# Both self attentions: ScalarE and VectorE share the copies of the projected values

## What is computed

```python
# first (sa): 16 heads of 16, rotary positions
q, k, v = jnp.split(layernorm(x) @ w_qkv, 3, axis=-1)
q = q * cos + rotate_half(q) * sin          # k likewise
attn = softmax(q @ k.T * scale)             # per sequence and head
x = x + (attn @ v) @ w_out + b_out
# second (sb): 8 heads, 64 wide for q and k, 32 wide for v
q, k = jnp.split(layernorm(x) @ W_qk, 2, axis=-1); v = layernorm(x) @ W_v
attn = softmax(q @ k.T * scale + conv[:, clipped_distance])
x = x + (attn @ v) @ W_out + b_out
```

## Time and profile before

| | us |
|---|---|
| median of 3 runs | 1342.28 (1341.74 to 1342.65) |
| the profiled execution | 1330.97 |
| its span, first to last instruction | 1329.2 |
| TensorE / VectorE / ScalarE / GpSimd busy | 1192.8 / 709.3 / 556.1 / 383.6 |
| value stage of `sa` (first matmul L785 to first of L798) | 862.3 to 875.1 |
| value stage of `sb` | 1182.3 to 1198.0 |

### The profile page before, as it was taken

One profiled execution on the slowest core, in us unless ns is written; L12 is line 12 of the kernel. 1 busy time (PEld: TensorE's weight loads), 2 busy tenths in 40 slices (PEclk: granted clock), 3 DMA queues, 4 the chain that ended last, 5 costly groups with the idle time before them and its releaser, 6 DMA issues. The chain is left out here.

```text
span 1329.2 us, 32322 instructions
## 1 busy us (share of the span) xinstructions
PE 1192.8 (90%) x13863; PEld 1048.1 (79%) x13863; DVE 709.3 (53%) x1127; ACT 556.1 (42%) x907; POOL 383.6 (29%) x339
## 2 busy tenths in 40 slices
PE   4799999999999999999999988796699999278799
PEld 4789889889889899899998977674477778266598
DVE  5555655565565575475475443275564222565732
ACT  4455555555555555555555532214532322111400
POOL 4632332332332342342242210053144000540000
PEclk9899999999999999999999985597989999589989
DMA  6937647647657556566665460190012121414045
GB/s 197 209 85 174 154 102 165 146 116 159 138 132 149 132 140 141 132 145 137 141 149 124 104 128 1 54 363 2 1 68 87 57 64 48 127 28 191 2 176 194
DMA packets 61732, 161.47 MB, mean 121 GB/s; under 512 B 24904, under 2 KB 38296, under 8 KB 58520
## 3 DMA queue, kind: packets, MB, share of 16 engines
q1 hardware_dynamic: 58904, 154.18, 46.0%
q0 software_dynamic: 1536, 4.20, 0.9%
q10 hardware_dynamic: 1152, 1.05, 0.2%
HBM read 70.56 MB, written 9.44 MB: 60 GB/s over the span
## 5 line engine op out<-in xcount | busy, mean ns | idle before, releaser
L366 ACT ACTIVATE xa_pt<-xa_sc 128x1024 f32<-128x1024 f32 (+1 forms) x224 | 212.4, 962 | 151.2 <-PE xa_sc L558 151.1
L412 DVE TENSOR_REDUCE xa_mx<-xa_sc 128x2 f32<-128x804 f32 x256 | 243.4, 991 | 41.4 <-PE xa_sc L542 41.4
L558 PE MATMUL xa_sc<-xa_queries,xa_keys 104*128 104x128 f32 (+1 forms) x1664 | 232.5, 285 | 2.4 <-DVE xa_queries L427 1.8
L558 PEld LDWEIGHTS xa_sc<-xa_queries,xa_keys 104*128 104x128 f32 (+1 forms) x1664 | 206.6, 196 | 21.0 <-issue 8.4
L479 PE MATMUL xa_pj<-xa_ctx_hi,xa_wk 128*128 128x400 f32 (+1 forms) x512 | 157.0, 349 | 0.9 <-DVE xa_qst L440 0.9
L479 PE MATMUL xa_pj<-xa_wv,xa_ctx_hi 128*128 128x256 f32 (+1 forms) x832 | 155.3, 286 | 0.1
L542 PE MATMUL xa_sc<-xa_keys,xa_queries 96*128 96x402 f32 x512 | 138.0, 373 | 13.0 <-DMA xa_keys<-xa_kst_hi 7.3
L569 PE MATMUL xa_op<-xa_pt,xa_values 128*32 128x64 f32 x6656 | 141.8, 228 | 7.7 <-ACT xa_pt L366 3.3
L295 POOL TENSOR_TENSOR xa_ctx_lo<-xa_raw,xa_ctx_hi 128x1600 fp32r<-128x1600 f32 (+1 forms) x32 | 115.9, 3623 | 78.0 <-DVE xa_ctx_hi L405 75.4
L300 POOL TENSOR_TENSOR xa_kst_lo<-xa_wk,xa_kst_hi 128x400 fp32r<-128x400 f32 x64 | 67.3, 1051 | 227.4 <-ACT xa_kst_hi L345 227.4
L479 PEld LDWEIGHTS xa_pj<-xa_wv,xa_ctx_hi 128*128 128x128 f32 (+1 forms) x832 | 126.2, 185 | 8.0 <-issue 6.5
(11 more groups left out here) (286 smaller groups left out, 1736.7 us busy)
## 6 DMA issues: line engine op xcount, KB each, us to landing
xa_keys<-xa_kst_hi SPq DMA_DIRECT2D x256, 200.2 KB, 6.1
xa_keys<-xa_kst_lo SPq DMA_DIRECT2D x128, 200.2 KB, 5.4
xa_raw<-in_ctxT SPq DMA_DIRECT2D x15, 1601.0 KB, 9.0
gf_w<-in_gf_w SPq DMA_DIRECT2D x16, 1024.0 KB, 7.1
moe_ex<-in_moe_ex SPq DMA_DIRECT2D x8, 1088.0 KB, 15.9
xa_queries<-xa_qst SPq DMA_DIRECT2D x96, 32.0 KB, 3.5
moe_slots_in<-in_moe_zero SPq DMA_DIRECT2D x1, 2944.0 KB, 16.4
moe_xs<-moe_slots_in SPq DMA_DIRECT2D x23, 128.0 KB, 2.2
```

Source lines behind the costliest of these rows:

```text
L366: nc.scalar.activation(PT[ptslot(step)][0:rows, 0:nt], SC[bank(step)][0:rows, 0:nt], ACT.Exp, scale=float(D0) ** -0.5).then_inc(ex_done, 1)
L412: nc.vector.tensor_reduce(mx[:, u // 2, 2 * (u % 2):2 * (u % 2) + 2], SC[bank(step)][:, :, 0:MXN], AX.X, ALU.max).then_inc(mx_done, 1)
L558: last = mm(SC[bank(step)][0:rows, kk, a * P:(a + 1) * P], KS[:, 2 * a + h, kt * P:kt * P + rows], QS[b % 2][:, 2 * a + h, :], start=True, ...
```

## The change

In both self attentions VectorE copies the even units only, and ScalarE the odd ones, with a semaphore of its own, `v_free`. Units 1 and 3 come after one half of `lnH` each, units 5 and 7 after the first and the second of `WH`. VectorE makes a half of `lnL` after units 0 and 2. TensorE waits for `v_free` ahead of odd units and for `pj_free` ahead of even ones; `pj_free` now counts 4 and not 8 for the values, so the later thresholds change. Ahead of unit 1 ScalarE also waits for zeros and ones. The diff without its unchanged surroundings:

```diff
-ATTENTION_SEMS = ("ln_hi", "ln_lo", "w_hi", "w_lo", "pj", "pj_free", "rot", ...
+ATTENTION_SEMS = ("ln_hi", "ln_lo", "w_hi", "w_lo", "pj", "pj_free", "v_free", "rot", ...
         def projected(eng, half):
-            eng.wait_ge(pj_free, T + half * (nproj // 2))
+            eng.wait_ge(pj_free, T // 2 + half * (nproj // 2))
             if rope:
                 eng.wait_ge(rot_done, half * (nproj // 4))
+        def values_of(n, e):
+            r_ = slice(e * S, (e + 1) * S)
+            return Vd[r_, 2 * n:2 * n + 2, :, e, 0:dv], PJ[n % 2][r_, 0:D].rearrange("p (b a v) -> p b a v", b=2, v=dv)
...
             for n in range(T):
-                ge(pe, pj_free, n - 1)
+                ge(pe, v_free if n % 2 else pj_free, n // 2)
...
                 n = T + m
-                pe.wait_ge(pj_free, n - 1)
+                pe.wait_ge(v_free if m == 1 else pj_free, T // 2 + max(m - 1, 0))
...
-            for n in range(T):
+            for n in range(0, T, 2):
                 dve.wait_ge(pj, n + 1)
                 for e in range(2):
-                    r_ = slice(e * S, (e + 1) * S)
-                    last = nc.vector.tensor_copy(Vd[r_, 2 * n:2 * n + 2, :, e, 0:dv],
-                                                 PJ[n % 2][r_, 0:D].rearrange("p (b a v) -> p b a v", b=2, v=dv))
+                    last = nc.vector.tensor_copy(*values_of(n, e))
                 last.then_inc(pj_free, 1)
-                if n % 2 and n // 2 < CH:
+                if n // 2 < CH:
                     k = n // 2
...
-                    dve.wait_ge(pj_free, n + 1)
+                    dve.wait_ge(pj_free, T // 2 + m + 1)
...
+            def values(n):
+                act.wait_ge(pj, n + 1)
+                if n == 1:
+                    for e in range(2):
+                        act.wait_ge(ones[e], 2)
+                for e in range(2):
+                    last = nc.scalar.activation(*values_of(n, e), ACT.Copy)
+                last.then_inc(v_free, 1)
             for k in range(CH):
                 nc.scalar.activation(lnH[:, k], lnT[:, k], ACT.Copy).then_inc(ln_hi, 1)
+                values(2 * k + 1)
             act.wait_ge(w_in, loaded)
-            for name in split_order:
+            for m, name in enumerate(split_order):
                 nc.scalar.activation(WH[name][:], W[name][:], ACT.Copy).then_inc(w_hi, 1)
+                if m < T // 2 - CH:
+                    values(2 * (CH + m) + 1)
```

More of the change, by code:

```diff
@@ L665, in add_bias @@
         nc.gpsimd.tensor_tensor(X[:, t], X[:, t], row[:], ALU.add).then_inc(added, 1)
-ATTENTION_SEMS = ("ln_hi", "ln_lo", "w_hi", "w_lo", "pj", "pj_free", "rot", "ones0", "ones1", "bias_added", "km_pool", "km_act", "v_in",
+ATTENTION_SEMS = ("ln_hi", "ln_lo", "w_hi", "w_lo", "pj", "pj_free", "v_free", "rot", "ones0", "ones1", "bias_added", "km_pool", "km_act", "v_in",
                   "s_full", "t_full", "o_full", "ot_full", "y_full", "mx", "sub", "exp", "t_ev", "rcp", "norm", "ot_ev", "y_ev", "stats")
@@ L715, in self_attention @@
         ln_hi, ln_lo, w_hi, w_lo = [sems[n] for n in ("ln_hi", "ln_lo", "w_hi", "w_lo")]
-        pj, pj_free, rot_done, bias_added, stats_done = [sems[n] for n in ("pj", "pj_free", "rot", "bias_added", "stats")]
+        pj, pj_free, v_free, rot_done, bias_added, stats_done = [sems[n] for n in ("pj", "pj_free", "v_free", "rot", "bias_added", "stats")]
         ones = [sems[f"ones{e}"] for e in range(2)]
```

## The result

The changed kernel took 1334.74 us (median of 4; 1333.53 to 1335.78), the kernel before 1342.10 in the same comparison: a ratio of 0.9947, 95% interval 0.9932 to 0.9962, which is 7.1 us (7.4 by the medians; the interval reaches from 5.1 to 9.1). The forecast was 6.3 us and 1336.0. Two later comparisons, on two chips (the chip of the first is not on record), gave 7.7 us (0.9942, 0.9927 to 0.9957) and 6.1 us (0.9954, 0.9942 to 0.9966).

What follows compares the result with a forecast made beforehand. TensorE's waits for VectorE's copies in both value stretches were taken as the bound to relieve. Gains of 2.4 (`sa`) and 3.9 us (`sb`) sum to 6.3, taking 1342.28 to 1336.0 us, range 1331.9 to 1340.5.

Steps and rivals of the forecast that it cites:

- What bounds it: Value stretches of both attentions: TensorE waits for VectorE's copies at L916, 3.7 us in `sa` and 5.6 in `sb`.
- Copies: Value stretches: sixteen of VectorE's 32 copies go to ScalarE, at 0.38 us each, 0.76 for a unit.
- `sa`: First attention's value stretch, replayed: queries can start at 872.75 us, 2.4 us earlier; 1.9 to 3.4 as ends.
- `sb`: Second attention's value stretch, replayed: queries at 1194.15 instead of 1198.03 us, 3.9 us earlier; 2.6 to 4.6 as ends.
- `lnL`: VectorE's low-half subtraction at L923 in `sa`: 1.23 us taken for the first, 1.67 for the second.
- The bound with 1.23 (2.8 us): `sa` replay variant: with 1.23 us for the second `lnL`, the gain is 2.8 us instead of 2.4.
- the replay: Value stretches of both attentions, stepped through in the new order with instruction durations taken from profile rows.
- GpSimd's queue: Behind `sa`'s value stretch: subtractions end by about 878 us, bias additions about 884.5; L891 can start at 885.5.
- The 11 us between profile and median: Whole kernel: the median shown lies 11 us above the profiled time, unexplained from the trace; assumed to cancel.
- The rivals: Clock takes 1.5 tiles, about 1339.7 us (0.11); ScalarE holds the banks (0.07); colder clock at first scores or tiles, 1346.8 (0.04).
- hold the banks: Value stretches: late ScalarE copies make TensorE wait for `v_free`, leaving some 2 us gain, 1340.3 us; chance 0.07.
- The sum: Both value stretches: 2.4 + 3.9 = 6.3 us gained, 4.5 and 8.0 as ends; median 1336.0 us.

Runs made afterwards that it cites:

- full: The full change run again on another chip, against the kernel before: 1321.24 us.
- pool_later: Kernel before, VectorE making all copies, but GpSimd's subtractions wait for both `lnL`: ratio 0.9976 against the kernel before, 3.2 us faster.
- lnl_last: Kernel before with both `lnL` moved behind the eighth unit: ratio 1.0037 against the kernel before, 4.9 us slower.
- before_again: The kernel before, unchanged, profiled once more: 1339.76 us, span 1338.0 us; no ratio.
- act_twice: Full change, but ScalarE copies each odd unit twice, first into a spare tile: 1325.33 us, ratio 0.9977 against the kernel before.
- `sa` alone: The change in the first attention only, against the kernel before: ratio 0.9995, and 0.9985 (2.0 us) when run again.

## Why the prediction was right, point by point

- *What bounds it.* Right. The stretch is set by VectorE's queue: half of the copies off it, and it shrinks (full); cheaper `lnL` in it, and it shrinks (pool_later); the same work in another order, and it doesn't (lnl_last).
- *Copies.* 0.79 us for a ScalarE unit, 0.76 taken from a row with twice the rows. Its single copy takes 377 to 397 ns with 64 rows, so 64 and 128 rows cost the same here.
- *`sa`.* 10.3 us against 10.4. Queries at 872.59 us, against 872.75.
- *`sb`.* 11.9 us from matmul to matmul against 11.9, with the tie between VectorE and `wl_q`, 0.3 us. The clock stayed full to the end of the stretch: the last pair no longer took 2.83 us.
- *`lnL`.* The term with an error. 1.67 us were taken for the second one in `sa` and it took 1.23, since `wh_q` was only ready when it ended. The bound with 1.23 (2.8 us) was the better one by this term. The result stayed at 2.5 because VectorE waited 0.25 us for the values of unit 2, which the replay had ready when the first `lnL` ended. That `sa` came out within 0.1 us is two small errors that cancel. What the prediction didn't say is how much the change owes to it: roughly half of the gain, 3.2 us with 1.4 either way, is to be had by GpSimd's order alone (pool_later). It was in the sum, as a lower price of `lnL`, but not named as a cause.
- *GpSimd's queue.* L891 was called the narrowest margin, about 1 us. It had 1.75 us of idle time ahead of it, against 10.45. GpSimd's additions now run beside more of VectorE's rotary additions, one of which took 1.21 us instead of 0.69; the query stretch in `sa` is 0.2 us longer, in each profile with the changed `sa`. That the one causes the other is not shown. This was not in the sum.

This is that row of the changed kernel, and the rotary addition:

```profile
881.77 1.21 DVE L944 TENSOR_TENSOR sa_KT<-sa_KT,sa_rot 128x512 f32<-128x512 f32 x1
...
885.34 4.83 POOL L896 TENSOR_TENSOR sa_Km<-sa_KT,consts 128x128 f32<-128x128 f32 x12 [1.75 <-DVE sa_KT L944]
```

- *The 11 us between profile and median.* The assumption that they cancel held, and this was luck, since the reason was not known: most likely the gap in the experts, which the profile of the changed kernel and that of before_again have. Whether the timed runs of the first comparison have it, no profile shows.
- *The rivals.* ScalarE did not hold the banks. By act_twice it would from about half a microsecond more per unit on (an estimate: the 0.78 us added to a unit, less the 1.0 us lost, over four handovers). The 2 us that this rival was to leave of the gain don't follow from its own terms: three handovers of 1.0 us each would take 3.0 us off each attention, all of the 2.4 and all but 0.9 of the 3.9. The time of the stages behind moved by up to 3.5 us between executions of the same program (131.9 to 135.4 "to scatter"), which is the width of the range; it may be why `sa` alone came out as low as 0.7 us. How much of this is the clock was not measured. Nothing went slower.
- *The sum.* The profile shows 2.5 + 3.8 = 6.3 us off the two stretches, as forecast, and the timed gain was 7.1, 7.7 and 6.1 us. What is above 6.3 is within the intervals.

## What to carry to other kernels

Where two banks pass between TensorE and an engine that also has long instructions of its own, add up that engine's whole queue in the stretch: if the sum is the stretch, only work taken off the queue helps, and a new order of the same work doesn't. Before moving work to another engine, look whether a long instruction is dear only because of a neighbour; here one wait on GpSimd gave roughly half of the gain. And beware of gathering short waits of TensorE into one long wait in front of a busy stretch: here the clock fell in a wait of 4 us, in both attentions, and it cost 5 us.

## What the runs showed of the hardware that was not expected

- A subtraction of two SBUF tensors of 128 x 1024 on VectorE costs 1.225 us alone and up to 2.995 us when it starts during a subtraction of GpSimd: it ends 1.08 us after GpSimd's instruction, however early it started in it. GpSimd's next instruction pays in turn: in the kernel before, `wl_k` in `sa` took 2.25 us instead of 1.27 and ended 1.12 us after `lnL`. The Trainium skill ("GPSIMD Engine Reference", section "Specifications") names contention with VectorE instructions that have two SBUF inputs; that section gives no price, and the trace agrees with it.
- On one kernel, two chips differ from a third by 11 us, and the profiles of the third have a gap of about 10 us in which TensorE executes next to nothing. TensorE waits in it for VectorE and VectorE for ScalarE, and ScalarE starts on a full bank only 22.9 to 23.0 us after GpSimd's first scatter in each of the five profiles that have the gap, 10 to 11 us late, with nothing in the profile that holds it. Two profiles are comparable only once such a gap is found in both or in neither.
